# A normalising pass on ScalarE in the first stage, and rows of tiles 0 to 11 carried on inside two nucleus steps of a four-layer graph network

## The reference, cut to what matters

```python
h = jnp.maximum(_layernorm(x, axis=-1), 0.0)
x = x + _L0_gnn_ref(h, adj, adj, Wq, Wk, Wv, Wout)      # attention
h = jnp.maximum(_layernorm(x, axis=-1), 0.0)
x = x + _L1_gnn_ref(h, adj, W1, W2, W3, U1, U2, U3, gamma, beta)
...
# inside _L1_gnn_ref
for s in range(2):                       # STEPS
    Q, K = Xa @ W1, Xa @ W3
    logits = Q @ W2 @ K.T
    # keep, per row, the largest entries until their softmax mass passes 0.9
    A = softmax(where(keep, logits, -inf))
    Xf = Rf @ Xf                         # forward diffusion by adj + I
    Xb = Rb @ Xb                         # backward diffusion
    Xa = A @ Xa                          # adaptive product
    Z = Z + (Xf @ U1[s] + Xb @ U2[s] + Xa @ U3[s])
```

## Time and profile before

| | |
|---|---|
| median of three runs | 3580.87 us |
| the profiled execution's own time | 3579.35 us |
| its span, first to last instruction | 3577.4 us |
| PE busy | 2916.8 us (82%) |
| DVE busy | 2320.2 us (65%) |
| ACT busy | 1276.1 us (36%) |
| mean granted TensorE clock | 0.923 of full |

### The profile page before, as it was taken

The page is one execution under the profiler, slowest core; times in us unless marked ns, Lnnn a source line. Parts: engine busy times, 40 slices in busy tenths (PEclk is TensorE's granted clock), DMA queues, the critical chain, the costliest instruction groups (busy, mean ns, idle before and its releaser), DMA issues. The chain is left out here.

```text
span 3577.4 us, 57809 instructions
## 1 busy us (share of the span) xinstructions
PE 2916.8 (82%) x20312; PEld 2138.2 (60%) x20312; DVE 2320.2 (65%) x4566; ACT 1276.1 (36%) x1644; POOL 50.2 (1%) x68
## 2 busy tenths in 40 slices
PE   1469999999999999999999566885677468686599
PEld 1346666767667676676766244664545356575488
DVE  6965556555565555555555599789587988895430
ACT  4643433444333443434433222332213343421211
POOL 0000000000000000000000100000000000000110
PEclk9579999999999999999999788997888789898899
DMA  5946748386583856838477110100011000110500
GB/s 216 374 160 169 184 111 197 97 195 165 130 198 96 200 132 160 202 92 199 118 170 188 50 47 24 60 31 18 1 45 36 1 25 24 36 36 4 218 1 25
DMA packets 586123, 396.75 MB, mean 111 GB/s; under 512 B 538371, under 2 KB 551174, under 8 KB 560390
## 3 DMA queue, kind: packets, MB, share of 16 engines
q1 hardware_dynamic: 584262, 382.49, 39.3%
q10 hardware_dynamic: 1728, 12.58, 1.1%
HBM read 223.05 MB, written 37.75 MB: 73 GB/s over the span
## 5 line engine op out<-in xcount | busy, mean ns | idle before, releaser
L675 DVE SCALAR_TENSOR_TENSOR e_lo<-e,e_hi 128x2048 f16<-128x2048 f32 x128 | 293.2, 2291 | 444.0 <-ACT e_hi L600 444.0
L554 PE MATMUL av<-vw_hi,pT_hi 128*128 128x256 f16 x2048 | 559.7, 273 | 5.9 <-DMA pT_lo<-e_lo 5.9
L554 PE MATMUL av<-vw_hi,pT_lo 128*128 128x256 f16 x2048 | 559.9, 273 | 0.0
L554 PE MATMUL av<-vw_lo,pT_hi 128*128 128x256 f16 x2048 | 559.8, 273 | 0.0
L543 PE MATMUL logits<-kT_hi,qT_hi 128*128 128x512 f16 x1024 | 389.0, 380 | 7.9 <-DVE att_small L661 5.9
L1753 DVE SCALAR_TENSOR_TENSOR nuc_junk<-nuc_e,nuc_thr 128x2048 bf16<-128x2048 f32 x168 | 388.4, 2349 | 4.7
L543 PE MATMUL logits<-kT_lo,qT_hi 128*128 128x512 f16 x1024 | 388.1, 379 | 0.0
L543 PE MATMUL logits<-kT_hi,qT_lo 128*128 128x512 f16 x1024 | 388.1, 379 | 0.0
L594 ACT ACTIVATE att_small<-att_small,minus 128x1 f32<-128x1 f32 x128 | 37.7, 295 | 830.2 <-DVE att_small L670 830.2
L661 DVE CUSTOM_DVE_ANT_0 e<-logits,bias,att_small 128x1024 f32<-128x1024 f32 x256 | 328.6, 1284 | 0.0
L595 ACT ACTIVATE e<-e,att_small,sc 128x2048 f32<-128x2048 f32 x128 | 266.2, 2080 | 0.0
(11 more groups left out here) (394 smaller groups left out, 5777.2 us busy)
## 6 DMA issues: line engine op xcount, KB each, us to landing
bias<-bias_scratch SPq DMA_DIRECT2D x130, 1024.0 KB, 4.8
bias_scratch<-adj_bias SPq DMA_DIRECT2D x16, 1024.0 KB, 8.2
adjT_scratch<-adjT SPq DMA_DIRECT2D x16, 1024.0 KB, 7.6
nuc_at_hi<-adjT_scratch SPq DMA_DIRECT2D x32, 512.0 KB, 3.9
nuc_at_lo<-adjT_scratch SPq DMA_DIRECT2D x32, 512.0 KB, 4.8
adjT<-adjT_scratch SPq DMA_DIRECT2D x16, 1024.0 KB, 20.5
adj_rows<-in_adj_dram ACTq DMA_DIRECT2D x12, 1024.0 KB, 9.3
adj_rows<-in_adj_dram SPq DMA_DIRECT2D x4, 1024.0 KB, 7.9
```

Source lines behind the costliest of these rows:

```text
L554: last = nc.tensor.matmul(AV[par][:, :], PT[par][w][:, m, :], VW[x][:, m, :], start=(m == 0 and w == x == 0), stop=(m == T - 1 and w == 1))
L675: nc.vector.scalar_tensor_tensor(out=EL[:, :], in0=E[par][:, :], scalar=P_SCALE, in1=EH[:, :], op0=ALU.mult, op1=ALU.subtract).then_inc(lo ...
```

## The change

Four places are edited. First, `setup`: VectorE's 16 subtract-and-scale passes go. VectorE makes two columns per tile instead (16 times the inverse deviation, and minus the mean times that), and ScalarE does the whole normalising and rectifying in one pass with them as scale and bias. The transposes use eight banks, wait only for the four tiles they read, and are emptied by ScalarE before the weights' high parts. VectorE subtracts the low parts of `hT` in two portions: three behind the weights' extremes, five behind the scales.

Second, `refresh` gets `first`, the first quad that it turns and multiplies. qk1 is called with `first=3`: only tiles 12 to 15 pass through the logit products there. It still cuts all 16 tiles into parts.

Third, in the first nucleus step a new piece `after(n)` takes two tiles of `out` at a time (n = 0 to 5, tiles 0 to 11) through transposes, W1, W3 and W2 and writes the next step's `QT` and `KT` in place. Four of these stand behind the diffusion tiles ahead of `multiply(2, 0)`, two ahead of the last tiles. Fourth, in the second step `after(n)` takes one tile through the last factor, U3[1], onto `y`, for all 16 tiles: four ahead of `logits(3, 0)`, four ahead of `multiply(2, 0)`, four ahead of the last tiles, the other four behind the products of the last tiles. The stage u3 goes. U3[1] is loaded at the start of that step.

```diff
-                for t in range(T):
-                    nc.vector.tensor_scalar(hx[:, t, :], hx[:, t, :], mv[:, t, 0:1], rstd[:, t:t + 1],
-                                            ALU.subtract, ALU.mult).then_inc(centred, 1)
+                link(nc.vector.tensor_scalar(rstd[:, :], rstd[:, :], H_SCALE, None, ALU.mult))
+                nc.vector.scalar_tensor_tensor(out=minus[:, :], in0=mv[:, :, 0], scalar=-1.0, in1=rstd[:, :],
+                                               op0=ALU.mult, op1=ALU.mult).then_inc(aimed, 1)
...
+                for b in range(3):
+                    remainder(b)
                 v.wait_ge(largest, 1)
...
                 v.wait_ge(powers, 1)
+                for b in range(3, 8):
+                    remainder(b)
...
+                s.wait_ge(aimed, 1)
+                for t in range(T):
+                    nc.scalar.activation(hx[:, t, :], hx[:, t, :], ACT.Relu, bias=minus[:, t:t + 1], scale=rstd[:, t:t + 1]).then_inc(rectified, 1)
...
-                          logits=(w1, w2, w3, QT, KT), parts=Xp, rows=X_SCALE)
+                          logits=(w1, w2, w3, QT, KT), parts=Xp, rows=X_SCALE, first=3 * step)
...
-                phase(refresh, "u3", XA, XA, ident, halfp, weight=a["L1_gnn_U3"][1], onto=Y)
...
-                    for b in range(QUADS):
+                    for b in range(first, QUADS):
                         turned(b)
...
+        AFTER = (((), range(0, 4), range(4, 6)), (range(0, 4), range(4, 8), range(8, 12)))[step]
...
+                    if k == 0 and g:
+                        pe.wait_ge(c_done, sum(len(AFTER[n]) for n in range(g)))
...
+                def after(n):                                    # TensorE
+                    tiles = (2 * n, 2 * n + 1) if step == 0 else (n,)
+                    pe.wait_ge(out_s, tiles[-1] + 1)
+                    if n:
+                        pe.wait_ge(c_done, n)
+                    for k in range(KC):
+                        for m, t in enumerate(tiles):
+                            o = (k * len(tiles) + m) * P
+                            last = nc.tensor.transpose(TP[0][:, o:o + P], out[:, t, k * P:(k + 1) * P], ident[:, :])
+                    last.then_inc(c_tp, 1)
+                    pe.wait_ge(c_xt, n + 1)
+                    if step:
+                        for k in range(KC):
+                            nc.tensor.matmul(TP[1][:, 0:D], cT[:, k * P:(k + 1) * P], U[:, 3, k, :], start=(k == 0), stop=False)
+                        nc.tensor.matmul(TP[1][:, 0:D], ident[:, :], y[:, n, :], start=False, stop=True).then_inc(c_prod, 1)
+                        return
+                    for o, w in ((TP[1][0:64, 0:D], w1[:, :, :]), (TP[1][:, D:2 * D], w3x)):
+                        for k in range(KC):
+                            last = nc.tensor.matmul(o, w[:, k, :], cT[:, k * D:(k + 1) * D], start=(k == 0), stop=(k == 1))
+                    last.then_inc(c_prod, 1)
+                    pe.wait_ge(c_read, 2 * n + 1)
+                    nc.tensor.matmul(TP[0][:, 0:D], w2x, QT[0:64, n * D:(n + 1) * D], start=True, stop=True).then_inc(c_prod, 1)
...
                 for t in range(DIFFUSED[0], DIFFUSED[1]):
                     diffuse_tile(t)
+                for n in AFTER[0]:
+                    after(n)
                 logits(3, 0)
...
+                def after(n):                                    # ScalarE
+                    s.wait_ge(c_tp, n + 1)
+                    if step:
+                        nc.scalar.activation(cT[:, :], TP[0][:, 0:D], ACT.Copy).then_inc(c_xt, 1)
+                        s.wait_ge(c_prod, n + 1)
+                        nc.scalar.activation(y[:, n, :], TP[1][:, 0:D], ACT.Copy).then_inc(c_done, 1)
+                        return
...
                     product(3, k)
+                    if step and k:
+                        after(LAST + k - 1)
+                if step:
+                    after(T - 1)
```

More of the change, by code:

```diff
@@ L1298, in _ @@
                     if logits is not None:
[L1299 to L1300 removed]
+                        pe.wait_ge(q_read, 2 * (QUADS - first))
+                        for b in range(first, QUADS):
                             nc.tensor.matmul(TP[b // 2][b % 2][:, :], w2x, QT[0:64, b * BANK:(b + 1) * BANK],
@@ L1310, in _ @@
                             nc.scalar.activation(dst[:, t, :], dst[:, t, :], ACT.Relu).then_inc(ready, 1)
[L1311 to L1316, removed]
+                    if turn and not first and 1 <= b <= QUADS:
+                        turned_copies(b - 1)
                     if parts and b >= 2:
@@ L1368, in _ @@
                 for b in range(QUADS):
-                    if turn:
+                    if turn and b >= first:
                         read(b)
@@ L1375, in _, with nucleus @@
                 if logits is not None:
-                    for b in range(QUADS):
-                        v.wait_ge(w2_s, b + 1)
+                    for b in range(first, QUADS):
+                        v.wait_ge(w2_s, b - first + 1)
                         nc.vector.tensor_copy(QT[:, b * BANK:(b + 1) * BANK], TP[b // 2][b % 2][:, :]).then_inc(w2_read, 1)
-def nucleus(nc, sb, ps, sem, name, QT, KT, parts, out, ident, diffusion):
+def nucleus(nc, sb, ps, sem, name, QT, KT, parts, out, ident, diffusion, next_logits):
     weights, at_d, scales, ident16, y, sc, Xp, Xf, Xb, step = diffusion
@@ L1606, in _ @@
                     diffuse_tile(t)
+                for n in AFTER[1]:
+                    after(n)
                 for k in range(G):
@@ L1610, in _ @@
                     diffuse_tile(t)
+                for n in AFTER[2]:
+                    after(n)
                 last_tiles()
```

87 lines of the change are left out of this document (52 added, 35 removed).

## The result

The changed kernel takes 3525.14 us, the median of four executions, against 3581.11 us for the kernel before on the same chip: a ratio of 0.9838, 95% interval 0.9823 to 0.9852. Predicted were 3545 us with a range of 3536 to 3561. The profiled execution took 3525.11 us (before: 3579.35).

A forecast was written before the change was run, and what follows sets the result against it. VectorE was taken to hold the first stage and the nucleus steps' ends, TensorE the pace around tile 12; -12.1 - 16.5 - 17.7 + 11.1 - 1.0 = -36.2 us from 3580.9 gave 3545 us, range 3536 to 3561.

The forecast's parts named there:

- First nucleus step: Six turns laid into TensorE's waits of 29.3 and 22.1 us in the first nucleus step: price 0, at worst 1 us.
- The sign that the prediction gave for this step: In the changed kernel's profile TensorE would still wait over 5 us before the last tiles of the first nucleus step.
- The turn's price: One turn of `after` in the first nucleus step: 4.9 us, or 7.5 us if TensorE ran at half rate throughout.
- Rival A: Turns run at half TensorE rate, 4.3 us each in the second nucleus step; sum -16.2, 3565 us; chance 0.12.
- First stage: Normalising moved to ScalarE and low parts reordered in `setup`: VectorE's last instruction ends near 57.6, a gain of 12.1 us.
- The normalising pass with two column operands: ScalarE's 16 passes in the first stage: 6.1 to 7.5 us, perhaps 9, hidden with 3 us to spare.
- qk1: Stage between the nucleus steps, copying one quad instead of four: ends at 2587.0 against 2603.5, a gain of 16.5 us.
- Second step with u3: Second nucleus step and the former u3 stage together, with 16 turns of 2.9 us each: predicted difference -7.6 us.
- The delay at tile 12: Second nucleus step: four turns ahead of tile 12's logits delay its maximum and VectorE's later cuts by 11.1 us.
- the tail of 5.3 us behind the last product: End of second nucleus step: a copy, 1.66 and 0.38 us for tile 14, and a whole turn for tile 15.
- eight turns stay hidden with 3 us to spare: Later in the second nucleus step: eight turns, 23.2 us, come out of TensorE's 26.6 us of waiting.
- 1.0 for the clock: Second step's last tiles: TensorE no longer idles before them, so its clock gains 1 us, between 0 and 2.

## Why the prediction was wrong

**First nucleus step: the failed step.** The prediction put the turns at "Price 0, at worst 1", and it put nothing at all for what the new first stage does to this step. "Four make 20 us in a hole of 29.3, two 10 us in one of 22.1. Nothing waits for them but TensorE." The fit was right (the kernel with everything but the new first stage shows it, 528.8 us) and the hole was not there. The argument took the hole as a property of the program's order, but it was the time of a branch that the data decides, and the same change altered the data. The rows could have said so: the earlier trace rows has VectorE busy for 27.2 of these 30 us, and I used that to say that it works, without asking at what. The lines are those of `release`, and a branch met once in four groups needs the question what decides it. The branch was worth 36.8 us; the turns, with only 15.6 us left to stand in, cost 19.3; together -17.4. The sign that the prediction gave for this step, a wait of over 5 us ahead of the last tiles, did not come: that wait is gone.

**The turn's price** was 4.9 us and is 5.2 at full clock, a fair reading. With everything at half rate I had 7.5 us. Rival A came true in part in this step: in four of the six turns the first eight products run at half rate and the turn takes 6.7 us or so. It came true in none of the second step's turns, where the clock is 0.98 to 1.00 and a turn takes 3.0 us (predicted 2.9). The rule of the Trainium skill on long waits between single matmuls (TensorE: Matmul & The Clock Gate, Loop structure matters more than you think) agrees with four turns of the first step and not with the second. The waits in a turn are for ScalarE and short here, 0.5 to 1.1 us.

**First stage**: 12.6 us for 12.1. The normalising pass with two column operands was bounded at 6 to 9 us and took 8.0, hidden. The Trainium skill's rule that rectifying, adding and multiplying belong on VectorE (ScalarE: Activation LUTs, Rules for kernel authors) gives as its reason a speed in bf16; x is f32 here. Keeping the subtracting and scaling on VectorE was tried, with the rectification on ScalarE as before, and cost 5.1 us, the 5 that were worked out. The choice of engine also decided whether the tie branch ran, which the sum had nowhere.

**qk1**: 17.0 for 16.5. **Second step with u3**: 8.1 for 7.6. The delay at tile 12, 10.2 us more waiting for the 11.1 forecast, and the tail of 5.3 us behind the last product were right. Wrong was the reading that eight turns stay hidden with 3 us to spare: TensorE waits no more before the last products (0.3 us in all), and VectorE's longest wait for it there is 4.0 us instead of 2.6. It cost little because the delay before had already moved VectorE back. Two small errors cancel here, which is luck: the last products start 11.4 us later in the step where 11.1 were forecast, but 10.2 of them are the delay at tile 12 and 1.2 are turns that were to be hidden. The products themselves take 4.0 us more where 5.0 were forecast (two turns of 3.0 less 1.0 for the clock), and what follows gives 23.5 where 23.7 were.

**Open**: one execution in four or so of some versions is 8 to 10 us shorter (3515.46 of the changed kernel), none of them profiled. The 1.3 us in `onward` and `last` lie within what that stretch varies between kernels that don't differ in it (251.4 to 255.5).

## What to carry to other kernels

Before a hole on one engine is used as cover, read which instructions of the other engine fill it, and whether a branch decides that they run. Where control flow depends on values, an edit that changes the last bits of an input can move more time than the edit itself. It could do so either way, and with other data it could come back, which no run here tries: the 36.8 us here belong to this input and this rounding, not to the design. A round trip of small products pays when it is overlapped with the next one; as a chain it costs both engines' latencies and, in four of the six turns of one step here, half the clock for a part of it.

## What the runs showed of the hardware

Multiplying and adding with two columns on VectorE seems not to give bit for bit what ScalarE's scale and bias with the same columns give: with the one the tie branch runs (20 replacements), with the other not (16), and nothing else differs in their arithmetic. The values themselves were not compared. ScalarE's pass with two column operands over 128x256 comes every 0.49 us (7.97 for 16). ScalarE's strided write of 128x256 into `KT` takes 0.62 us where the plain copy takes 0.38. Sixteen transposes take 3.51 us behind a pause of 15.6 us, in a stretch of 6 us whose granted clock is 0.73, and 2.05 us without the pause. Five float32 products at the end of a diffusion tile take 4.20 us in one kernel (granted clock 0.50) and 2.52 in another (1.00) at the same place of the same list.
